# One layer norm in place of two, and block roundings moved between the first projections

## The chip, the cores and the metric

The kernel runs on one core of a Trainium2 chip. The core has five engines that run side by side and meet only at semaphores: PE (TensorE, matrix products and transposes), DVE (VectorE), ACT (ScalarE), POOL (GpSimd) and SP (SyncE, which here only issues transfers). The metric is the device time of one execution in microseconds (us).

## The reference, cut to what matters

One decoder block: a gated cross-attention, then a gated mixture of experts. Only the way into the attention matters here.

```python
def _ln(x, w, b):
    mu = jnp.mean(x, axis=-1, keepdims=True)
    var = jnp.mean(jnp.square(x - mu), axis=-1, keepdims=True)
    return (x - mu) * jax.lax.rsqrt(var + EPS) * w + b          # EPS = 1e-5

def _div_clamp_fp8(x, scale):
    y = jnp.clip(x / scale, -448, 448).astype(bfloat16).astype(float32)
    return y.astype(float8_e4m3fn).astype(float32)

x = x + tanh(g_xattn[0]) * xattn(layernorm(x), ctx_2048, ...)   # layernorm: no w, b
x = x + tanh(g_ffn[0]) * ffn(layernorm(x), ...)

def xattn(hidden, cond, ...):
    ln_out = _ln(hidden, ln_w, ln_b)            # a second normalisation of a normalised row
    q  = _ln(fp8_linear(ln_out, wq,  q_in_scale))       # qx, k, v alike
    ...
```

x is 4 blocks of 256 rows of 256 columns. Every linear input is divided by a scale of its own (q, k, v, qx), rounded to bf16 and then to fp8.

## The kernel before, in words

The program is written by hand: each engine has its own instruction list, in order, and waits on semaphores. After a start, a loop of 34 steps (`for i in range(NSUB + MAXLAG)`) runs the attention, software-pipelined: step i projects the queries of sub-step i (`project_q`), scores and exponentials of i - 1, products of i - 2. Then come the router and the experts. The change touches only the start, the loop's step 0 and one place of step 2; the loop itself and what follows stay.

The start, for each of the four blocks b of x (two tiles of 128 rows):

- SP loads x (L390), fifteen vectors into rows of one tile (L401), the context (L432), the weights of the first group (L404) and eight scalars, each spread over 128 partitions (L437). All leave in this order on one queue.
- `ln_step` on DVE, for two normalisations: statistics (`bn_stats`, `bn_aggr`, L963 to L969), POOL raises the variance to -0.5 (`ln_rstd`, L506), DVE scales (L954). The order over blocks and normalisations is written out in `LN_STEPS`.
- PE turns the vectors to columns (L1412; `vectors()` on DVE takes them over, L974) and transposes the normalised block (`transpose_h`, L1370). ACT multiplies by weight and bias (`ln_out`, L661) and divides by the four scales into bf16 (`quant_y`, L671).
- `quant` on DVE rounds to fp8 with a magic number: clamp (L992), exponent bits (L993), magic (L994), add (L995). `quant_sub` on POOL subtracts the magic again, into `xq` in 32 bits (L512). Two buffers serve the four blocks (`q_y[b % 2]`), so block b waits for the subtraction of block b - 2.
- PE transposes the first weights (`fill_kv`, L1388/L1390; two banks, so the third fill waits for the first to be emptied); ACT and DVE split them into a high and a low part (`kv_hi` L684, `kv_lo` L1016; `wq_hi` L698, `wq_lo` L1030); the context likewise (`ctx_hi` L652, `ctx_lo` L1001).
- `project_kv(0, 0)` (L1441, L1450) and `project_kv(0, 1)` follow for the keys and values of block 0, `project_q(0)` (L1465) for its queries. Each is normalised by the same round: squares on ACT (L733 for keys, L740 for queries), sums on DVE (`sums`, L1068), power on POOL (`rstd_kv`, `rstd_q`, L525/L529), scaling on DVE (`scaled_kv` L1077, `scaled_q` L1088). PE transposes the result (`fill_Tq` L1479, `fill_Tk` L1491), and DVE writes the low parts of queries and keys (`qk_lo`, L1098).

Where the roundings stand in DVE's list before:

```python
sums(0, 4)
quant(1)
scaled_kv(0, 0)
wq_lo(0, 0); wq_lo(1, 0)
# step 0:  sums(key 1), quant(2), wq_lo(0, 1), scaled_kv(0, 1), wq_lo(1, 1),
#          sums(query 0), quant(3), scaled_q(0), qk_lo(keys), qk_lo(queries) ...
```

and the order in which ACT starts: `ln_out(0)`, `quant_y(0)`, `ctx_hi(0)`, `ctx_hi(1)`, four `kv_hi`, `ctx_hi(2)`, `ctx_hi(3)`, `ln_out(1)`, `quant_y(1)`, two Tanh of the gates (L715, L716), squares of the first keys, `wq_hi`, `evac_v`, `ln_out(2)`, `ln_out(3)`, `quant_y(2)`, and in step 0 `quant_y(3)`.

Of the kernel before, what the change touches and what calls it, by code (L numbers as in the profile page):

```python
# [5 lines left out]
def flamingo_kernel(nc: bass.Bass, t: dict, out: bass.AP):  # L6
# [4 lines left out]
    ALU = mybir.AluOpType  # L11
# [4 lines left out]
    P = 128  # L16
# [9 lines left out]
    EPS = 1e-5  # L26
# [18 lines left out]
    with ctx:  # L45
# [340 lines left out]

        @block.sync
        def _(sp):
            for b in range(NB):
# [4 lines left out]
            for name, row in (("L0_xattn_ln_w", 0), ("L0_xattn_ln_b", 2), ("L0_xattn_q_in_scale", 4),  # L394
                              ("L0_xattn_k_in_scale", 6), ("L0_xattn_v_in_scale", 8),
                              ("L0_xattn_qx_in_scale", 10), ("L0_xattn_qln_w", 12), ("L0_xattn_qln_b", 13),
                              ("L0_xattn_qxln_w", 14), ("L0_xattn_qxln_b", 15), ("L0_xattn_kln_w", 16),
                              ("L0_xattn_kln_b", 17), ("L0_xattn_kxln_w", 18), ("L0_xattn_kxln_b", 19),
                              ("L0_xattn_proj_smooth", 20)):
                n = t[name].shape[0] // P  # L400
                sp.dma_start(vec_rows[row:row + n, :], t[name].rearrange("(r p) -> r p", p=P)).then_inc(vec_loaded, 16)  # L401
# [89 lines left out]
        def _(pool):  # L491
# [9 lines left out]
            def ln_rstd(count):  # L501

                pool.wait_ge(var8_ready, count + 1)
                b = LN_STATS[count][1]
# [61 lines left out]
            for i in range(NSUB + MAXLAG):  # L566
# [7 lines left out]
                if i == 0:  # L574
                    quant_sub(2)
# [7 lines left out]
                if i == 0:  # L583
                    quant_sub(3)
# [63 lines left out]
        def _(act):  # L648
# [62 lines left out]
            ln_out(1)  # L711
            quant_y(1)

            act.wait_ge(scal_loaded, 16 * len(SCALARS))
            nc.scalar.activation(gate[:, 0:1], scal[:, 6:7], ACT.Tanh).then_inc(gate_ready, 1)  # L715
            nc.scalar.activation(gate[:, 2:3], scal[:, 7:8], ACT.Tanh).then_inc(gate_ready, 1)  # L716
# [221 lines left out]
        def _(dve):  # L938
# [8 lines left out]
            def ln_step(scale, i, b):  # L947

                src = (x_sb, h_sb)[i]
                tiles = range(TPB * b, TPB * (b + 1))  # L950
                if scale:
                    dve.wait_ge(rstd8_ready, LN_STATS.index((i, b)) + 1)
                    for n in tiles:
                        ins = nc.vector.tensor_scalar(h_sb[:, n, :], src[:, n, :], mv[:, n, 0:1], rs8[:, n:n + 1],  # L954
                                                      ALU.subtract, ALU.mult)
                    ins.then_inc(h_ready, 1)
                else:
                    if i == 0:
                        dve.wait_ge(x_loaded[b], 16)
                    else:  # L960
                        dve.wait_ge(h_ready, [st[1:] for st in LN_STEPS if st[0]].index((0, b)) + 1)
                    for n in tiles:
                        ins = nc.vector.bn_stats(stat[:, n, :], src[:, n, :])  # L963
                    link(ins)
                    for n in tiles:
                        ins = nc.vector.bn_aggr(mv[:, n, :], stat[:, n, :])
                    link(ins)
                    nt = slice(TPB * b, TPB * (b + 1))
                    nc.vector.tensor_scalar_add(mv[:, nt, 1], mv[:, nt, 1], EPS).then_inc(var8_ready, 1)  # L969
# [17 lines left out]
            def quant(b):  # L987
# [5 lines left out]
                link(nc.vector.tensor_scalar(mg.bitcast(U16), y.bitcast(U16), 0x7F80, None, ALU.bitwise_and))  # L993
# [801 lines left out]
```

## Time and profile before

| | |
|---|---|
| median of 3 runs | 809.79 us (809.17 to 809.99) |
| the profiled execution | 810.1 us, span 808.3 us |
| busy share of the span | PE 90%, DVE 75%, ACT 58%, POOL 57% |
| mean granted PE clock | 0.967 of full |

The span runs from the first to the last instruction of the profiled execution; the time of that execution also holds what lies around it. A busy share is an average over the whole run; a stage has its own.

### The profile page before, as it was taken

How to read it: one execution, taken by the hardware profiler on the slowest of the kernel's cores; microseconds unless marked ns; L12 is line 12 of the kernel's file. 1: busy time of each engine (PE TensorE's matmuls, PEld its weight loads, DVE VectorE, ACT ScalarE, POOL GpSimd, SP SyncE). 2: the span in 40 equal slices, each digit the busy share in tenths (PEclk: the TensorE clock that was granted, in tenths of full speed). 3: DMA queues.
4: the chain of work that ended last, by engine and by line, in shares of the span. 5: the costliest groups of instructions: out<-in, count | busy, mean ns of one | idle time of the engine just before them, and what ended most of it. 6: DMA issues, size and time to landing. Idle time of an engine off the chain costs nothing.

```text
span 808.3 us, 15347 instructions
## 1 busy us (share of the span) xinstructions
PE 724.2 (90%) x4857; PEld 588.7 (73%) x4857; DVE 607.9 (75%) x1312; ACT 466.1 (58%) x1178; POOL 458.4 (57%) x592
## 2 busy tenths in 40 slices
PE   3548999899999989999998999998978788999996
PEld 2547778687888878888887788887766555777775
DVE  6866888788888878889886978988887673445544
ACT  3655767667686776768676776866654222222221
POOL 3464777666777766677775667676766223222220
PEclk9778999999999999999999999999999796999999
DMA  5320000101000010000001010000001104666661
GB/s 184 96 67 1 27 28 1 40 30 38 1 27 28 1 54 27 27 2 27 28 1 53 2 34 1 27 1 2 1 13 48 64 3 119 196 194 189 196 187 53
DMA packets 44478, 42.74 MB, mean 53 GB/s; under 512 B 3717, under 2 KB 43386, under 8 KB 44410
## 3 DMA queue, kind: packets, MB, share of 16 engines
q1 hardware_dynamic: 42874, 36.62, 14.9%
q0 software_dynamic: 1536, 5.28, 2.4%
q8 instruction: 35, 0.57, 0.3%
q14 instruction: 33, 0.27, 0.1%
HBM read 39.52 MB, written 2.37 MB: 52 GB/s over the span
## 4 chain that ended last, share of the span: by engine, by line
PE 61%; DVE 20%; issue 6%; ACT 6%; POOL 4%; SPq 2%; DMA 1%; POOLq 0%; DVEq 0%; ACTq 0%
PE out_ps L1729 9%; PE proj_ps L1465 6%; PE s_ps L1509 6%; PE pT_ps L1518 5%; PE proj_ps L1450 5%; DVE q_tok L1088 5%; PE aux_ps L1479 4%; PE aux_ps L1528 4%; PE aux_ps L1542 4%; PE proj_ps L1441 4%; PE work_ps L1721 3%; POOL rstd L529 3%; DVE pT_sb L1113 3%; DVE ss L1068 2%; PE work_ps L1743 2%
## 5 line engine op out<-in xcount | busy, mean ns | idle before, releaser
L544 POOL TENSOR_SCALAR p_sb<-p_sb,psum_row 128x256 f32<-128x256 f32 x256 | 125.1, 504 | 66.9 <-DVE psum_row L1107 65.7
L798 ACT ACTIVATE p_sb<-s_ps,negmax 128x256 f32<-128x256 f32 x256 | 118.2, 472 | 64.9 <-DVE negmax L1102 63.8
L1528 PE MATMUL aux_ps<-pT_sb,v_sb 128*128 128x512 f32 x256 | 120.7, 593 | 3.7 <-DVE pT_sb L1113 3.7
L1113 DVE COPY pT_sb<-pT_ps 128x512 f32<-128x512 f32 x128 | 87.7, 686 | 44.2 <-PE pT_ps L1518 43.8
L1509 PE MATMUL s_ps<-kT,qT 128*128 128x256 f32 x768 | 112.2, 289 | 8.3 <-DVE qT L1098 6.1
L551 POOL TENSOR_TENSOR y_bf<-y_bf,mg_bf 128x512 bf16<-128x512 bf16 x64 | 85.8, 1341 | 58.8 <-DVE mg_bf L1125 58.8
L1509 PEld LDWEIGHTS s_ps<-kT,qT 128*128 128x128 f32 x768 | 97.6, 190 | 18.4 <-issue 18.4
L1102 DVE TENSOR_REDUCE negmax<-s_ps 128x2 f32<-128x512 f32 x128 | 86.5, 683 | 5.9 <-PE s_ps L1509 5.6
L529 POOL TENSOR_TENSOR rstd<-var,minus_half 128x8 f32<-128x8 f32 (+1 forms) x64 | 86.6, 1353 | 5.5 <-POOL var L525 0.4
L554 POOL TENSOR_TENSOR catq<-y_bf,mg_bf 128x512 fp32r<-128x512 bf16 x64 | 79.5, 1242 | 5.0
L1729 PE MATMUL out_ps<-eo,onehot 128*128 128x256 f32 x512 | 74.4, 298 | 0.6 <-ACT eo L908 0.6
L1542 PE MATMUL aux_ps<-wpT,catq 128*128 128x256 f32 x512 | 69.1, 288 | 5.9 <-DVE wkvT L1019 4.8
L1518 PE MATMUL pT_ps<-ident,p_sb 128*128 128x128 f32 x512 | 72.9, 276 | 0.9 <-POOL p_sb L544 0.7
L1465 PE MATMUL proj_ps<-wqT,xq 128*128 128x256 f32 x512 | 69.6, 291 | 4.5 <-DVE k_tok L1077 4.5
L1729 PEld LDWEIGHTS out_ps<-eo,onehot 128*128 128x128 f32 x512 | 66.4, 194 | 9.9 <-issue 8.6
L638 POOL DMA_INDIRECT gx<-rows_dram,idx_cur x32 | 33.0, 1031 | 69.4 <-DVE w_slot L1312 60.0
L1465 PEld LDWEIGHTS proj_ps<-wqT,xq 128*128 128x128 f32 x512 | 66.2, 198 | 4.9 <-DVE wqT L1030 4.7
L1528 PEld LDWEIGHTS aux_ps<-pT_sb,v_sb 128*128 128x128 f32 x256 | 44.0, 190 | 35.1 <-issue 35.1
L1542 PEld LDWEIGHTS aux_ps<-wpT,catq 128*128 128x128 f32 x512 | 63.2, 190 | 6.8 <-DVE wkvT L1019 5.5
L1068 DVE TENSOR_REDUCE ss<-sq 128x8 f32<-128x1024 f32 (+1 forms) x64 | 60.5, 945 | 7.7 <-ACT sq L733 3.9
L1518 PEld LDWEIGHTS pT_ps<-ident,p_sb 128*128 128x128 f32 x512 | 60.5, 142 | 6.6 <-POOL p_sb L544 2.5
L908 ACT ACTIVATE eo<-work_ps,w_slot 128x256 fp32r<-128x256 f32 x32 | 15.1, 473 | 82.9 <-PE work_ps L1743 82.9
(180 smaller groups left out, 1406.8 us busy)
## 6 DMA issues: line engine op xcount, KB each, us to landing
w_up_a<-in_L_ffn_gate_up_proj SPq DMA_DIRECT2D x16, 384.0 KB, 3.6
w_up_b<-in_L_ffn_gate_up_proj SPq DMA_DIRECT2D x16, 384.0 KB, 3.5
wp_raw<-in_L_xattn_wproj SPq DMA_DIRECT2D x16, 256.0 KB, 2.9
w_down_a<-in_L_ffn_down_proj SPq DMA_DIRECT2D x16, 192.0 KB, 3.6
w_down_b<-in_L_ffn_down_proj SPq DMA_DIRECT2D x16, 192.0 KB, 3.6
w_raw<-in_L_xattn_w_kv_x SPq DMA_DIRECT2D x8, 256.0 KB, 4.1
w_raw<-in_L_xattn_wq SPq DMA_DIRECT2D x7, 256.0 KB, 2.7
w_raw<-in_L_xattn_wqx SPq DMA_DIRECT2D x7, 256.0 KB, 3.0
```

The lines of the kernel that those rows point to most:

```text
L529: nc.gpsimd.tensor_tensor(rstd[:, at], var8[:, at], minus_half[:, 0:w], ALU.pow).then_inc(rstd_ready, 1)
L544: ins = nc.gpsimd.tensor_scalar(p_sb[:, r, st, :], p_sb[:, r, st, :], rsum[:, r, st:st + 1], 1.0, ALU.mult, ALU.mult)
L551: nc.gpsimd.tensor_tensor(yc_bf[:, ty, :], yc_bf[:, ty, :], mg_bf[:, ty, :], ALU.add).then_inc(catq_ready, 1)
L798: ins = nc.scalar.activation(p_sb[:, r, st, :], s_ps[:, r % 2, st, :], ACT.Exp, bias=negmax[:, r, st:st + 1], accum_out=psum_row[:, r, st: ...
L1102: nc.vector.tensor_reduce(negmax[:, r, :], s_ps[:, r % 2, :, :], AX.X, ALU.max, negate=True).then_inc(max_ready, 1)
L1113: nc.vector.tensor_copy(pT_sb[:, r // 2, r % 2, :, :], pT_ps[:, r % 2, :, :]).then_inc(pT_ready, 1)
L1465: ins = nc.tensor.matmul(proj_ps[:, t, x * 256:(x + 1) * 256], xq[:, s.b, 3 * x, c, t * P:(t + 1) * P], wqT[:, s.gi, part, c, x * 256:(x + ...
L1509: ins = nc.tensor.matmul(s_ps[:, k % 2, st, :], qT[:, a, ty, h, st * P:(st + 1) * P], kT[:, b, ty, s.gi, :], start=(i == 0), stop=(i == 2))
L1518: ins = nc.tensor.transpose(pT_ps[:, r % 2, tt, st * P:(st + 1) * P], p_sb[:, r, st, tt * P:(tt + 1) * P], ident[:, :])
L1528: ins = nc.tensor.matmul(aux_ps[:, f.bank, :], v_sb[:, (2 * s.n + tt) % VRING, ty, s.gi, :], pT_sb[:, ty, :, tt, :], start=(tt == 0), stop ...
L1542: ins = nc.tensor.matmul(aux_ps[:, f.bank, tt * H:(tt + 1) * H], catq[:, s.gi, blk, tt * P:(tt + 1) * P], wpT[:, s.gi, part, blk, :], star ...
L1729: ins = nc.tensor.matmul(out_ps[:, n, :], onehot[:, u % 2, n * P:(n + 1) * P], eo[:, part, :], start=False, stop=False, skip_group_check=True)
```

## The change

- One normalisation in place of two. With v the variance of x, the second normalisation of a normalised row is the first with (v + EPS)^-0.5 replaced by (v (1 + EPS) + EPS^2)^-0.5, so statistics, power and scaling are done once per block.
- SP sends two blocks of x, seven vectors, the other two blocks, the keys' and values' weights, then the context. ACT's own queue sends the other eight vectors and the eight scalars, before ACT's first work. A one-column activation with no use of its own follows them.
- ACT does `ln_out` and `quant_y` of blocks 0 and 1 at the start, of block 2 after the context, and `ln_out(3)` ahead of the loop; the two Tanh move into step 2. `evac_v(0, 0)` goes ahead of `wq_hi`. PE transposes blocks 2 and 3 earlier.
- `quant` is cut into `quant_exponents` and `quant_round`, which stand in other places of DVE's list; those of block 3 now stand ahead of the query sums. The magic of blocks 2 and 3 is subtracted on DVE (`quant_less`) in place of POOL.

```diff
+        VECTORS = [... ln_w, ln_b, four in_scales, proj_smooth, then eight query and key vectors]
+        def load_vectors(eng, vectors):
+            for name, row in vectors:
+                n = t[name].shape[0] // P
+                eng.dma_start(vec_rows[row:row + n, :], t[name].rearrange("(r p) -> r p", p=P)).then_inc(vec_loaded, 16)
...
+            load_x(0)
+            load_x(1)
             sp.wait_ge(rows_clear, 1)
-            for name, row in ((fifteen vectors)):
-                ...
+            load_vectors(sp, VECTORS[:7])
+            load_x(2)
+            load_x(3)
...
+            load_kv(0, 0)
             sp.dma_start(ctx_raw, ...)
-            load_kv(0, 0)
             load_kv(0, 1)
             load_wq(0, wq0_raw, wq0_loaded)
-            for i, name in enumerate(SCALARS):
-                sp.dma_start(scal[:, i:i + 1], t[name].partition_broadcast(P)).then_inc(scal_loaded, 16)
... POOL
-            for count in range(7):
-                ln_rstd(count)
+            for b in range(NB):
+                ln_rstd(b)
             quant_sub(0)
-            ln_rstd(7)
...
-                if i == 0:
-                    quant_sub(2)
...
-                if i == 0:
-                    quant_sub(3)
... ACT
+            act.wait_ge(rows_clear, 1)
+            load_vectors(act, VECTORS[7:])
+            for i, name in enumerate(SCALARS):
+                act.dma_start(scal[:, i:i + 1], t[name].partition_broadcast(P)).then_inc(scal_loaded, 16)
+            act.wait_ge(memset_done, 3)
+            nc.scalar.activation(gate[:, 3:4], minus_half[:, 0:1], ACT.Identity)
             ln_out(0)
             quant_y(0)
+            ln_out(1)
+            quant_y(1)
             ctx_hi(0)
             ctx_hi(1)
...
             ctx_hi(3)
-            ln_out(1)
-            quant_y(1)
-            act.wait_ge(scal_loaded, 16 * len(SCALARS))
-            (two Tanh)
+            ln_out(2)
+            quant_y(2)
...
             squares_kv(0, 0)
+            evac_v(0, 0)
             wq_hi(0, 0)
             wq_hi(1, 0)
-            evac_v(0, 0)
-            ln_out(2)
             ln_out(3)
-            quant_y(2)
...
+                if i == 2:
+                    act.wait_ge(scal_loaded, 16 * len(SCALARS))
+                    (two Tanh)
... DVE
+            def ln_stats(b):
+                ... (bn_stats, bn_aggr of x_sb)
+                nc.vector.tensor_scalar(mv[:, nt, 1], mv[:, nt, 1], 1.0 + EPS, EPS * EPS, ALU.mult, ALU.add
+                                        ).then_inc(var8_ready, 1)
+            def ln_norm(b):
+                dve.wait_ge(rstd8_ready, b + 1)
+                ... (tensor_scalar of x_sb into h_sb, two tiles)
...
+            def quant_less(b):
+                dve.wait_ge(z_ready, b + 1)
+                dve.wait_ge(xq_ready, b)
+                nc.vector.tensor_tensor(xq[:, b, :, :, :].rearrange("p a c k -> p (a c) k"), q_y[b % 2], q_mg[b % 2],
+                                        ALU.subtract).then_inc(xq_ready, 1)
...
-            for step in LN_STEPS[:7]:
-                ln_step(*step)
+            ln_stats(0)
+            ln_stats(1)
+            ln_norm(0)
             vectors()
-            for step in LN_STEPS[7:12]:
-                ln_step(*step)
+            ln_norm(1)
+            ln_stats(2)
+            ln_stats(3)
+            ln_norm(2)
+            ln_norm(3)
             weight_scales()
-            quant(0)
+            quant_exponents(0)
+            quant_round(0)
             ctx_lo(0)
...
-            for step in LN_STEPS[12:]:
-                ln_step(*step)
...
+            quant_exponents(1)
+            quant_round(1)
             sums(0, 4)
-            quant(1)
+            quant_exponents(2)
             scaled_kv(0, 0)
             wq_lo(0, 0)
             wq_lo(1, 0)
+            quant_round(2)
             for i in range(NSUB + MAXLAG):
...
                 if i == 0:
-                    quant(2)
+                    quant_less(2)
...
+                if i == 0:
+                    quant_exponents(3)
+                    quant_round(3)
+                    quant_less(3)
                 if s0:
                     sums(q_seq(s0.a), 8)
-                if i == 0:
-                    quant(3)
... PE
             for i in range(2):
                 transpose_ctx(i)
+            transpose_h(2)
             for c, x in KV_ORDER:
                 fill_kv(c, x, 0)
             for i in range(2, 4):
                 transpose_ctx(i)
+            transpose_h(3)
...
             project_kv(0, 0)
-            transpose_h(2)
-            transpose_h(3)
```

## Rows read from the trace of the kernel before

**Rows 1.** Busy time by stage: us, then PE, PEld, DVE, ACT, POOL, clock, DMA.
```profile
0.00:68.80 68.80, 34.60 (x182) 30.74 (x182) 50.28 (x114) 37.49 (x84) 31.93 (x32) 0.85 0.33 102
```

**Rows 2.** The chain of waits in order of time: start, us, what.
```profile
15.25 3.46 DMA scal<-in_g_ffn
```

**Rows 3.** Timeline of SP's queue at the start: start, us, transfer issued.
```profile
3.19 0.25 SPq L401 DMA_DIRECT2D sq<-in_L_xattn_ln_b  x1
...
7.02 0.32 SPq L401 DMA_DIRECT2D sq<-in_L_xattn_proj_smooth  x1
...
11.76 0.60 SPq L437 DMA_DIRECT2D scal<-in_L_xattn_wq_scale  x1
```

**Rows 4.** Timeline of ACT, start to 50 us; brackets: idle before, releaser.
```profile
11.56 1.28 ACT L661 ACT_TABLE_LOAD   x1 [11.56 <-PE s_ps L1370]
12.86 1.02 ACT L661 ACTIVATE acc<-s_ps,vec 128x256 f32<-128x256 f32 x2
...
17.12 1.05 ACT L652 ACTIVATE ctxT<-pT_ps 128x512 fp32r<-128x512 f32 x2
...
33.47 0.19 ACT L715 ACTIVATE gate<-scal 128x1 f32<-128x1 f32 x1
...
33.66 0.57 ACT L733 ACTIVATE sq<-proj_ps 128x512 f32<-128x512 f32 x1
...
48.27 0.47 ACT L698 ACTIVATE wqT<-aux_ps,wscale 128x256 fp32r<-128x256 f32 x1
```

**Rows 5.** Timeline of DVE, start to 64 us.
```profile
5.75 0.73 DVE L954 TENSOR_SCALAR pT_sb<-x_sb,q_tok 128x256 f32<-128x256 f32 x2
...
19.27 0.68 DVE L992 TENSOR_SCALAR wp_raw<-wp_raw 128x2048 bf16<-128x2048 bf16 x1
...
21.44 1.22 DVE L995 TENSOR_TENSOR wp_raw<-wp_raw,qk_f 128x2048 bf16<-128x2048 bf16 x1
...
23.18 1.65 DVE L1016 SCALAR_TENSOR_TENSOR wkvT<-aux_ps,wscale,wkvT 128x256 fp32r<-128x256 f32 x4
...
28.62 1.43 DVE L1001 TENSOR_TENSOR ctxT<-pT_ps,ctxT 128x512 fp32r<-128x512 f32 x2 [0.16 <-ACT ctxT L652]
...
38.18 0.68 DVE L1077 TENSOR_TENSOR k_tok<-proj_ps,rstd 128x512 f32<-128x512 f32 x1
...
53.86 1.22 DVE L1068 TENSOR_REDUCE ss<-sq 128x8 f32<-128x1024 f32 x1 [3.85 <-ACT sq L740]
...
58.31 1.22 DVE L1088 TENSOR_TENSOR q_tok<-proj_ps,rstd 128x1024 f32<-128x1024 f32 x1
59.44 3.65 DVE L1098 TENSOR_TENSOR kT<-qk_f,kT 128x512 fp32r<-128x512 f32 x1
```

**Rows 6.** Timeline of PE, start to 60 us.
```profile
8.76 0.45 PE L1412 MATMUL proj_ps<-ident,sq 128*128 128x128 f32 x1 [8.76 <-DMA sq<-in_L_xattn_proj_smooth]
...
24.20 1.19 PE L1388 MATMUL aux_ps<-center,w_raw 128*128 128x128 f32 x4 [5.95 <-DVE wkvT L1016]
...
38.97 2.04 PE L1441 MATMUL proj_ps<-wkvT,xq 128*128 128x256 f32 x8 [2.87 <-DVE k_tok L1077]
...
59.58 1.11 PE L1479 MATMUL aux_ps<-ident,q_tok 128*128 128x128 f32 x4 [6.38 <-DVE q_tok L1088]
```

**Rows 7.** Timeline of POOL, start to 77 us.
```profile
0.75 0.20 POOL L492 MEMSET sq<- 128x128 f32 x1 [0.29 <-POOLq L1783]
...
35.69 1.46 POOL L529 TENSOR_TENSOR rstd<-var,minus_half 128x4 f32<-128x4 f32 x1
...
38.34 4.08 POOL L512 TENSOR_TENSOR xq<-v_sb,y_bf 128x2048 fp32r<-128x2048 bf16 x1 [1.19 <-DVE v_sb L995]
...
75.23 1.65 POOL L529 TENSOR_TENSOR rstd<-var,minus_half 128x8 f32<-128x8 f32 x1
```

**Rows 8.** The page's costliest groups: count, busy us, mean ns, idle before.
```profile
L638 POOL DMA_INDIRECT gx<-rows_dram,idx_cur x32 | 33.0, 1031 | 69.4 <-DVE w_slot L1312 60.0
```

**Rows 9.** Busy time by stretches of 4 us, columns as in rows 1.
```profile
56.00:60.00 4.00, 0.42 (x2) 0.42 (x3) 3.93 (x5) 0.00 (x0) 3.43 (x2) 0.50 0.17 58
```

More of the change, by code:

```diff
@@ L385, in qk_parts, with load_x @@
             return qk_f[:, 0, :], [qT[:, part, int(x == "TX"), :, :].rearrange("p a b -> p (a b)") for part in range(2)]
+        VECTORS = [("L0_xattn_ln_w", 0), ("L0_xattn_ln_b", 2), ("L0_xattn_q_in_scale", 4), ("L0_xattn_k_in_scale", 6),
+                   ("L0_xattn_v_in_scale", 8), ("L0_xattn_qx_in_scale", 10), ("L0_xattn_proj_smooth", 20),
+                   ("L0_xattn_qln_w", 12), ("L0_xattn_qln_b", 13), ("L0_xattn_qxln_w", 14), ("L0_xattn_qxln_b", 15),
+                   ("L0_xattn_kln_w", 16), ("L0_xattn_kln_b", 17), ("L0_xattn_kxln_w", 18), ("L0_xattn_kxln_b", 19)]
+        def load_vectors(eng, vectors):
+            for name, row in vectors:
+                n = t[name].shape[0] // P
+                eng.dma_start(vec_rows[row:row + n, :], t[name].rearrange("(r p) -> r p", p=P)).then_inc(vec_loaded, 16)
         @block.sync
         def _(sp):
-            for b in range(NB):
+            def load_x(b):
                 sp.dma_start(x_sb[:, TPB * b:TPB * (b + 1), :], t["x"][b, :, :].rearrange("(n p) h -> p n h", p=P)
                              ).then_inc(x_loaded[b], 16)
+            load_x(0)
+            load_x(1)
             sp.wait_ge(rows_clear, 1)
[L394 to L401, printed above, removed]
+            load_vectors(sp, VECTORS[:7])
+            load_x(2)
+            load_x(3)
             def load_rows(dst, name, row, n, done):
@@ L499, in _, with ln_rstd @@
                                         base=0, pattern=[[-1, P]], channel_multiplier=1).then_inc(const_ready, 1)
-            def ln_rstd(count):
-                pool.wait_ge(var8_ready, count + 1)
-                b = LN_STATS[count][1]
+            def ln_rstd(b):
+                pool.wait_ge(var8_ready, b + 1)
                 nt = slice(TPB * b, TPB * (b + 1))
@@ L710, in _ @@
             ctx_hi(3)
-            ln_out(1)
-            quant_y(1)
-            act.wait_ge(scal_loaded, 16 * len(SCALARS))
-            nc.scalar.activation(gate[:, 0:1], scal[:, 6:7], ACT.Tanh).then_inc(gate_ready, 1)
-            nc.scalar.activation(gate[:, 2:3], scal[:, 7:8], ACT.Tanh).then_inc(gate_ready, 1)
+            ln_out(2)
+            quant_y(2)
             def wp_hi(ty, g):
@@ L853, in _ @@
                     quant_y(3)
+                if i == 2:
+                    act.wait_ge(scal_loaded, 16 * len(SCALARS))
+                    nc.scalar.activation(gate[:, 0:1], scal[:, 6:7], ACT.Tanh).then_inc(gate_ready, 1)
+                    nc.scalar.activation(gate[:, 2:3], scal[:, 7:8], ACT.Tanh).then_inc(gate_ready, 1)
                 if s1:
@@ L945, in link @@
                 dve.wait_ge(dve_chain, chain[0])
-            def ln_step(scale, i, b):
-                src = (x_sb, h_sb)[i]
+            def ln_stats(b):
                 tiles = range(TPB * b, TPB * (b + 1))
[L951 to L957, printed above, removed]
-                    if i == 0:
[L959 to L969, printed above, removed]
+                dve.wait_ge(x_loaded[b], 16)
+                for n in tiles:
+                    ins = nc.vector.bn_stats(stat[:, n, :], x_sb[:, n, :])
+                link(ins)
+                for n in tiles:
+                    ins = nc.vector.bn_aggr(mv[:, n, :], stat[:, n, :])
+                link(ins)
+                nt = slice(TPB * b, TPB * (b + 1))
+                nc.vector.tensor_scalar(mv[:, nt, 1], mv[:, nt, 1], 1.0 + EPS, EPS * EPS, ALU.mult, ALU.add
+                                        ).then_inc(var8_ready, 1)
+            def ln_norm(b):
+                dve.wait_ge(rstd8_ready, b + 1)
+                for n in range(TPB * b, TPB * (b + 1)):
+                    ins = nc.vector.tensor_scalar(h_sb[:, n, :], x_sb[:, n, :], mv[:, n, 0:1], rs8[:, n:n + 1],
+                                                  ALU.subtract, ALU.mult)
+                ins.then_inc(h_ready, 1)
             def vectors():
@@ L985, in weight_scales, with quant_exponents @@
                 ins.then_inc(wscale_ready, 1)
-            def quant(b):
+            def quant_exponents(b):
                 y, mg = q_y[b % 2], q_mg[b % 2]
@@ L1364, in transpose_h @@
             def transpose_h(b):
-                pe.wait_ge(h_ready, [st[1:] for st in LN_STEPS if st[0]].index((1, b)) + 1)
+                pe.wait_ge(h_ready, b + 1)
                 wait(pe, yT_ready, b - 1)
```

6 lines of the change are left out of this document (2 added, 4 removed).

## The prediction, made before the changed kernel was run

> **What bounds the kernel now.** I read the stages first: up to 68.80 us PE, which elsewhere bounds this kernel, works only 34.60 us [rows 1]. So the start is a chain of hand-overs, and only the start is edited. Then the chain of waits: it goes through SP's queue, which issues one transfer after another until the last scalar leaves at 15.25, and the scalar's landing ends the wait of DVE [rows 2]. SP's own timeline shows why: 13 issues of vectors take from 3.19 to 7.02, 0.295 us each, and the scalars begin only at 11.76, 0.50 us each to 15.25 [rows 2, 3]. Last, the four engines: ACT's first work, a table load, starts at 11.56, its first `ln_out` at 12.86 and the next job at 17.12 [rows 4]; DVE rounds block 0 from 19.27 to 22.66 and only then gives PE's second half of the weights its bank, at 24.20 [rows 5, 6]; the sums of squares of the first queries start at 53.86, and their transposes at 59.58 [rows 5, 6]. The reader is to see that each start hangs on the end of another engine's work: what the change is worth is how much earlier PE starts at 59.58.
>
> **The change, step by step.** The sum is a timetable of the new order, from durations of before.
>
> *ACT free.* ACT now issues 8 vectors and 8 scalars itself, after POOL's clearing memset (0.75 + 0.20, so 1.0 [rows 7]). No row shows an issue on ACT. The nearest are SP's: 8 x 0.295 + 8 x 0.50 = 6.36, mean 0.40. The far bounds are the vectors' 0.295 for all (1.6 us less) and POOL's indirect transfers, 1.03 each [rows 8]. I take SP's, which are the same transfers. Then the table load 1.28 and a one-column activation, 0.19 like the Tanh [rows 4]: ACT is free at 1.0 + 6.36 + 1.47 = 8.8.
>
> *Does its input wait?* `ln_norm(0)` needs what it needed: 5.75 + 0.73 = 6.48 [rows 5]. The second statistics, powers and scalings, which stood between this and the transposes, are gone. PE's transpose of the vectors (0.45, at 8.76 before, 1.7 us after proj_smooth's issue at 7.02 [rows 3, 6]) now needs an issue at about 3.7, so it can run at 5.5. The four transposes of block 0 (1.11, as for four at 59.58 [rows 6]) end at 7.7. ACT's 8.8 is later and sets the start. x's third and fourth blocks, now behind seven vectors, and the context behind wk and wv are needed later still; DVE's normalisations of all four blocks end by about 12 and are covered by ACT.
>
> *First weights.* ACT runs `ln_out` and `quant_y` of two blocks: 17.12 - 12.86 = 4.26 each [rows 4], to 17.3. Two context copies, 17.12 to 18.17 before, take it to 18.4. Then `kv_hi` at once, as the scalars landed 3.5 us after their last issue at 7.3 (before: from 15.25 to 18.7 [rows 2]). The halves of a block are 0.42 each like `kv_lo`'s 1.65 for four [rows 5], so `kv_hi(0,0)` ends at 19.2, `kv_lo(0,0)` at 20.1, and PE starts at 20.25 in place of 24.20 [rows 6]: -3.95. DVE no longer rounds block 0 just before this; that sits at 13.1 to 16.5, in ACT's shadow.
>
> *First squares.* From PE's 24.20 to ACT's squares at 33.66 the same work follows: fills, copies, one `ln_out`, one `quant_y`. The two Tanhs before the squares (33.47 to 33.66 [rows 4]) are gone: -4.15, squares at 29.5. `quant_exponents(1)` and `quant_round(1)`, now ahead of the sums, start when the context subtractions end (28.62 + 1.43 - 3.95 = 26.1 [rows 5]), take 3.4 (four steps, 19.27 to 22.66 [rows 5]), end at 29.5, and are done as the squares end at 30.1. Without that cover the sums move by the difference.
>
> *First keys.* The power ended at 35.69 + 1.46 = 37.15 [rows 7], but DVE, busy with the rest of quant(1), scaled only at 38.18 [rows 5]. Now it is ready: 37.15 - 4.15 = 33.0, -5.1 for `scaled_kv(0,0)` and PE's 38.97 [rows 6], now 33.85.
>
> *Rounding block 2.* POOL's `quant_sub(1)` (4.08 [rows 7]) runs from 33.1 to 37.2. DVE's copy of the keys with both inputs in SBUF took 3.65 us beside POOL's last such subtraction, 59.44 to 63.09, where a normal one is 0.68 [rows 5]: I let `quant_round(2)` wait until 37.2 and end at 39.1. `sums` follow to 39.8. Then `quant_less(2)`, new on DVE. Its wait for `quant_sub(1)` is over by then; behind it in the queue are `wq_lo(0,1)`, `scaled_kv(0,1)` and so `project_q(0)`. Its price is in no row. Below it is the addition of the same size in bf16, 1.22; above it POOL's 4.08. It writes 32 bits, so I take the 32-bit rate: 0.68 for 512 and 1.22 for 1024 elements [rows 5], 0.54 per 512, so 2.3 for 2048. It ends at 42.1. POOL's small power waits behind it (1.3 more), `scaled_kv(0,1)` ends at 44.1.
> The Trainium skill ("VectorE: DVE Perf Modes", What auto-detection actually checks) lets a two-input operation go at double rate only if every tensor is 16 bits wide, and so sides with 2.3; at 1.22 the sum would be 1.2 us better.
>
> *Rounding block 3.* ACT's second half of the query weights starts at 48.27 [rows 4], 5.1 earlier at 43.2, done at 44.0: about level with DVE. DVE's `wq_lo(1,1)` ends at 45.0, the roundings of block 3 at 48.4, `quant_less(3)` at 50.7, and all of this is now ahead of the query sums. They start at 50.7 in place of 53.86: the gain falls from 5.1 to 3.2. But nothing stands behind them: the sums end at 51.9, the power takes 2.15 with its preparation (1.65 undisturbed [rows 7]), `scaled_q(0)` starts at 54.05 in place of 58.31 [rows 5]. So -4.3, and PE's 59.58 becomes 55.3. From there the same loop follows. The 3.65 us of the keys disappears, but PE projected in those microseconds, so I count nothing for it.
>
> *Tanh in the loop.* The two Tanhs return in step 2, ahead of the query's first half, on ACT's way: +0.2.
>
> Sum: -4.1. Against the profiled execution (810.1; span 808.3 and 1.8 around it) 806.0; the median shown is 0.3 lower, so **805.7**. A measurement here can tell about 0.2%, 1.6 us, from no change.
>
> **Rivals.**
> 1. *ACT's issues are dear (the other side).* ACT's start sets the chain, so each extra microsecond counts fully. It matches before at 0.40 + 4.1/16 = 0.65 us per issue and is slower by 0.2% from 0.75 on. At POOL's 1.03 [rows 8] it is 16 x 0.63 = 10.1 worse: 815.8. [...] Against: the same descriptors from SP at 0.295 to 0.50. At a middling 0.6 it ends at 808.9, no change.
> 2. *Transfers, not issues, set the start.* If the vectors still land for a transpose at 8.76, ACT starts after 8.76 + 0.45 + 1.11 = 10.3, 1.5 later: 807.2. Against: SP's issues follow back to back, and the landing is 1.7 us after the last one. The Trainium skill ("DMA: Bandwidth & Descriptors", Issuing engines are not separate DMA queues) speaks for it: two issuing engines share the same transfer engines and save only issue time, usually small; here the rows show issue time of 12 us on SP, so I give it little.
> 3. *DVE's subtraction costs what POOL's did.* 4.08 in place of 2.3, twice on the way: +3.6, 809.3, no change. At 1.22 it is 1.1 to 1.2 better: 804.5.
> 4. *The clock.* PE's granted clock is 0.50 from 56 to 60 [rows 9], half of full, that is 1.2 in place of 2.4 GHz, after an idle stretch of 6 us before 59.58. I keep that: PE's wait before 55.3 is as long. If the tighter start kept it at 2.4 GHz, the two groups of transposes and the first projection would halve, about 1.5: 804.2. A loss of the same size would come from a projection that falls to the lower clock: 807.2.
>
> **How the numbers follow.** As summed, with the small clock shifts, 0.60; rival 2 0.10; a cheaper subtraction or a kept clock 0.15; rival 1 0.12, of which 0.08 to 0.6 or 0.7 us per issue, no change or near it, and 0.04 slower; rival 3's dear end 0.03. Faster takes the first three and 0.02 of the dear issues' lower part: 0.87; same 0.09; slower 0.04. The range leaves out the dear ends (0.11 above) and some of a double gain below (0.05): from 803.4, where the cheap subtraction and a kept clock come nearly together, to 808.4, where an issue costs 0.57 us.
>
> **What would show it.** In the changed profile: ACT's table load ends by 8.7 and `quant_y(0)` begins by 10; PE's second half of the weights near 20.3, the squares near 29.5, DVE's two subtractions near 2.3 us each, query sums near 50.7 and PE's first query transposes near 55.3; everything after by the same offset. The prediction is wrong if ACT's `ln_out(0)` comes after 12.9, if DVE's subtractions exceed 4 us, or if the offset at PE's query transposes isn't that of the end.

## The result and the profile after

The changed kernel took **802.85 us** (median of 4 runs, 801.96 to 804.23) against 809.88 for the kernel before on the same chip (4 runs): ratio 0.9923, 95% interval 0.9912 to 0.9935. It is faster by 7.0 us, where 4.1 were forecast. The profiled execution took 801.96 us, span 800.1, mean granted clock of PE 0.977 of full speed (before 0.967).

The stage in which the change lies, and another stretch further on, of the changed kernel (the row of 68.80 us answers to [rows 1], the next to [rows 9]; columns as there):

```profile
0.00:68.80 68.80, 36.66 (x211) 32.53 (x212) 49.87 (x93) 39.11 (x88) 22.66 (x30) 0.90 0.32 102
...
52.00:56.00 4.00, 1.51 (x7) 1.51 (x8) 1.82 (x2) 0.29 (x1) 1.18 (x1) 0.50 0.00 0
...
554.00:556.00 2.00, 2.00 (x19) 2.00 (x18) 1.38 (x4) 0.52 (x2) 1.44 (x4) 1.00 0.00 0
```

In the same 68.80 us PE does 211 products in place of 182. At its query transposes (52 to 56) it still has half the clock, 1.2 in place of 2.4 GHz.

The chain of waits of the changed kernel, in order of time, answers to [rows 2]; the scalars have left it, and the context's transfer stands in it:

```profile
6.11 8.63 DMA p_sb<-in_ctx
...
47.64 2.29 DVE xq L1005
```

SP's queue, then ACT's queue and ACT itself (answer to [rows 3] and [rows 4]):

```profile
3.73 0.32 SPq L391 DMA_DIRECT2D sq<-in_L_xattn_proj_smooth  x1
6.11 0.53 SPq L436 DMA_DIRECT2D p_sb<-in_ctx  x1
```

```profile
0.98 0.52 ACTq L391 DMA_DIRECT2D sq<-in_L_xattn_qln_w  x1
...
7.22 0.58 ACTq L700 DMA_DIRECT2D scal<-in_g_ffn  x1
7.83 1.28 ACT L702 ACT_TABLE_LOAD   x1 [7.83 <-issue]
...
9.23 1.00 ACT L656 ACTIVATE acc<-s_ps,vec 128x256 f32<-128x256 f32 x2
...
17.71 1.05 ACT L647 ACTIVATE ctxT<-pT_ps 128x512 fp32r<-128x512 f32 x2
...
28.74 0.58 ACT L732 ACTIVATE sq<-proj_ps 128x512 f32<-128x512 f32 x1
```

Sixteen issues on ACT take from 0.98 to 7.83, 0.43 each (forecast 0.40); `ln_out(0)` starts at 9.23 in place of 12.86. DVE (answer to [rows 5]):

```profile
34.50 2.33 DVE L998 TENSOR_SCALAR qk_f<-qk_f 128x2048 bf16<-128x2048 bf16 x1
38.60 2.28 DVE L1005 TENSOR_TENSOR xq<-wp_raw,qk_f 128x2048 fp32r<-128x2048 bf16 x1
...
47.64 2.29 DVE L1005 TENSOR_TENSOR xq<-v_sb,y_bf 128x2048 fp32r<-128x2048 bf16 x1
49.85 1.21 DVE L1082 TENSOR_REDUCE ss<-sq 128x8 f32<-128x1024 f32 x1
53.21 1.23 DVE L1102 TENSOR_TENSOR q_tok<-proj_ps,rstd 128x1024 f32<-128x1024 f32 x1 [2.15 <-POOL rstd L528]
54.35 0.68 DVE L1112 TENSOR_TENSOR kT<-qk_f,kT 128x512 fp32r<-128x512 f32 x1
57.18 0.69 DVE L1112 TENSOR_TENSOR qT<-qk_f,qT 128x512 fp32r<-128x512 f32 x1 [2.15 <-ACT qT L782]
```

PE (answer to [rows 6]; the last row belongs to step 29 of the loop) and POOL ([rows 7]):

```profile
6.75 0.45 PE L1431 MATMUL proj_ps<-ident,sq 128*128 128x128 f32 x1 [6.75 <-DMA sq<-in_L_xattn_proj_smooth]
...
14.79 1.97 PE L1398 MATMUL pT_ps<-ident,p_sb 128*128 128x128 f32 x8 [4.95 <-DMA p_sb<-in_ctx]
20.88 0.68 PE L1407 MATMUL aux_ps<-center,w_raw 128*128 128x128 f32 x4 [0.73 <-DVE wkvT L1027]
...
33.12 1.61 PE L1462 MATMUL proj_ps<-wkvT,xq 128*128 128x256 f32 x8 [4.08 <-DVE k_tok L1091]
...
54.49 1.12 PE L1500 MATMUL aux_ps<-ident,q_tok 128*128 128x128 f32 x4 [7.58 <-DVE q_tok L1102]
56.11 1.83 PE L1462 MATMUL proj_ps<-wkvT,xq 128*128 128x256 f32 x8
57.78 1.55 PE L1471 MATMUL proj_ps<-wkvT,ctxT 128*128 128x512 f32 x6
...
553.91 2.05 PE L1486 MATMUL proj_ps<-wqT,xq 128*128 128x256 f32 x16
```

```profile
32.21 4.07 POOL L512 TENSOR_TENSOR xq<-v_sb,y_bf 128x2048 fp32r<-128x2048 bf16 x1
38.89 2.06 POOL L524 TENSOR_SCALAR var<-ss 128x4 f32<-128x4 f32 x1 [2.61 <-DVE ss L1082]
```

POOL's indirect transfers, [rows 8], are the same (mean 1031 ns). To see where the time comes from, lay one event of every step of the loop beside its twin: the start of DVE's scaling of the queries, `scaled_q`. Before, it starts at 58.31 in step 0, 76.92 in step 1, 547.94 in step 28 and 602.62 in step 31. The changed kernel is 5.10 earlier in step 0, 6.67 in step 1, 6.39 in step 28, 7.84 in step 29 and 7.89 in step 31. So there are three portions: 5.1 us up to the first queries, 1.6 in step 1, and 1.45 in step 29, 500 us from anything edited. The base of these differences is one execution of the kernel before, of 810.1 us; its executions in the batches below go from 807.75 to 811.11, so a number in them can be a microsecond away from a difference of medians. The last portion shows in the kernel before as this projection (the same 16 products that take 2.05 above), and the stretch around it:

```profile
560.30 3.12 PE L1465 MATMUL proj_ps<-wqT,xq 128*128 128x256 f32 x16
```

```profile
560.00:562.00 2.00, 2.00 (x15) 2.00 (x15) 1.26 (x6) 0.91 (x4) 1.58 (x4) 0.73 0.00 0
562.00:564.00 2.00, 2.00 (x11) 2.00 (x11) 0.65 (x2) 0.55 (x1) 1.78 (x2) 0.50 0.00 0
```

Same order, same work, but clock 0.73 and 0.50 where the changed kernel had 1.00.

### The profile page after: what moved, and what is told of

It reads as the page before. It is cut to its first block, busy times and chain, and to the rows that moved or that the text cites. A ratio compares the mean times of both kernels' runs of the same rounds, so it can differ in the third digit from the quotient of the medians.

```text
span 800.1 us, 15318 instructions
## 1 busy us (share of the span) xinstructions
PE 718.0 (90%) x4857; PEld 582.8 (73%) x4857; DVE 604.1 (76%) x1286; ACT 466.1 (58%) x1179; POOL 447.4 (56%) x586
## 4 chain that ended last, share of the span: by engine, by line
PE 63%; DVE 18%; ACT 6%; issue 6%; POOL 4%; DMA 1%; SPq 1%; POOLq 0%; DVEq 0%; ACTq 0%
PE out_ps L1748 9%; PE s_ps L1530 6%; PE proj_ps L1486 6%; PE proj_ps L1471 6%; PE pT_ps L1539 5%; DVE q_tok L1102 5%; PE aux_ps L1549 4%; PE aux_ps L1500 4%; PE aux_ps L1563 4%; PE proj_ps L1462 4%; PE work_ps L1740 3%; POOL rstd L528 3%; DVE pT_sb L1127 3%; DVE ss L1082 3%; PE work_ps L1762 2%
## 5 line engine op out<-in xcount | busy, mean ns | idle before, releaser
L633 POOL DMA_INDIRECT gx<-rows_dram,idx_cur x32 | 33.0, 1031 | 69.0 <-DVE w_slot L1331 59.8
L1486 PE MATMUL proj_ps<-wqT,xq 128*128 128x256 f32 x512 | 67.0, 284 | 4.0 <-DVE k_tok L1091 4.0
L1486 PEld LDWEIGHTS proj_ps<-wqT,xq 128*128 128x128 f32 x512 | 63.6, 191 | 4.3 <-issue 4.3
L760 ACT ACTIVATE qk_f<-aux_ps,vec 128x512 f32<-128x512 f32 x64 | 49.8, 778 | 23.6 <-PE aux_ps L1500 21.0
```

The source lines that it names most:

```text
L1486: ins = nc.tensor.matmul(proj_ps[:, t, x * 256:(x + 1) * 256], xq[:, s.b, 3 * x, c, t * P:(t + 1) * P], wqT[:, s.gi, part, c, x * 256:(x + ...
```

## The experiments

The first theory: the new issue order (scalars off the end of SP's list) gives nearly all of the first portion, the second normalisation and the roundings' places nothing, and the other portions are TensorE's clock. In the table "earlier by" is the start of `scaled_q` in the kernel before minus that of the run, in us, from each run's profile; the medians of before stand in brackets.

| run | median, us | ratio, 95% | earlier by: step 0 | step 1 | step 28 | step 31 |
|---|---|---|---|---|---|---|
| changed kernel | 802.85 (809.88) | 0.9923, 0.9912 to 0.9935 | 5.10 | 6.67 | 6.39 | 7.89 |
| e1 | 809.16 (809.01) | 1.0, 0.9991 to 1.001 | 0.04 | 0.01 | 0.00 | 0.00 |
| e2 | 805.22 (809.01) | 0.9956, 0.994 to 0.9971 | 4.96 | 5.49 | 5.46 | 5.42 |
| e3 | 805.25 (809.01) | 0.9958, 0.9942 to 0.9974 | 5.11 | 5.75 | 5.50 | 5.44 |
| e4 | 802.12 (809.01) | 0.9911, 0.9896 to 0.9926 | 6.91 | 7.74 | 7.45 | 7.42 |
| e5 | 804.47 (809.26) | 0.9932, 0.9919 to 0.9944 | 4.95 | 5.17 | 4.97 | 4.96 |
| e6 | 802.97 (809.26) | 0.9926, 0.9913 to 0.994 | 4.49 | 6.14 | 5.93 | 7.44 |
| e7 | 806.35 (809.26) | 0.9968, 0.9955 to 0.998 | 2.56 | 4.26 | 3.98 | 5.45 |
| e8 | 803.18 (809.26) | 0.9923, 0.9911 to 0.9935 | 6.92 | 7.33 | 7.06 | 7.04 |
| e9 | 801.54 (809.11) | 0.9901, 0.9887 to 0.9914 | 7.09 | 8.17 | 7.92 | 7.92 |
| e10 | 799.38 (809.11) | 0.9882, 0.9867 to 0.9898 | 7.01 | 9.98 | 9.76 | 11.25 |
| e11 | 804.63 (809.11) | 0.9939, 0.992 to 0.9957 | 3.01 | 4.39 | 4.06 | 5.54 |

**e1: one normalisation alone**, in the order of before.

```diff
-        LN_STEPS = [(0, 0, 0), (0, 0, 1), (1, 0, 0), (0, 1, 0), (1, 0, 1), (0, 1, 1), ...]
+        LN_STEPS = [(0, 0, 0), (0, 0, 1), (1, 0, 0), (1, 0, 1), (0, 0, 2), (0, 0, 3), (1, 0, 2), (1, 0, 3)]
...
-                    nc.vector.tensor_scalar_add(mv[:, nt, 1], mv[:, nt, 1], EPS)
+                    nc.vector.tensor_scalar(mv[:, nt, 1], mv[:, nt, 1], 1.0 + EPS, EPS * EPS, ALU.mult, ALU.add)
...
```

> The kernel before with only its two normalisations made one; transfers, orders and roundings stay. Theory (the issue order holds the start): ACT could begin about 1 us sooner, but DVE's weight scales still wait for the last scalar, landing at 18.7, and the rounding of block 0 and the first weights stand behind them. PE's second half of the weights stays at 24.2 (within 0.3) and the time at 809.9, no change. Rival (the dropped normalisation is the gain): PE's 24.2 comes 2 us or more earlier and the time is 807.9 or less.

809.16 against 809.01: nothing. DVE only waits longer for the last scalar (4.13 us in place of 2.86), and the weight scales come at 18.70 (18.74 before). So the work that gave the change its name was covered.

**e2: the issue order alone.** The kernel before with SP's new order, and vectors and scalars issued by ACT ahead of its work; all else as before.

```diff
...
+            load_vectors(act, VECTORS[7:])
+            for i, name in enumerate(SCALARS):
+                act.dma_start(scal[:, i:i + 1], t[name].partition_broadcast(P)).then_inc(scal_loaded, 16)
...
```

> The kernel before with only the new issue order: SP's list, ACT's sixteen issues, the early one-column activation; both normalisations and the old places of the roundings stay. Theory: the scalars land by 13.4, but the second normalisation of block 0 still ends at 10.3, so ACT starts at 11.5; rounding of block 0 runs from 15.9 to 19.3, PE's second half of the weights starts at 21.0 in place of 24.2, and the rest follows by 3.2: 806.7. Rival (transfers, not issues, set the start): within 0.5 of 809.9. Rival (the normalisation is the gain): the same.

4.96 at step 0, as much as the first portion of the changed kernel, and 3.8 us in the median; 3.2 were expected. The second half of the weights came about where it was expected (21.24); 1.8 more came between it and the squares, which start 7.64 behind it, at 28.88, in place of 9.46. PE's second half of the weights, at 24.20 before [rows 6]:

```profile
21.24 0.68 PE L1399 MATMUL aux_ps<-center,w_raw 128*128 128x128 f32 x4 [1.66 <-DVE wkvT L1027]
```

**e3: the roundings in their old places**, the rest of the change in.

```diff
                 if s0:
                     sums(q_seq(s0.a), 8)
+                if i == 0:
+                    quant_exponents(3)
+                    quant_round(3)
...
+                if i == 0:
+                    quant_sub(2)   # and (3), on POOL as before
```

> The changed kernel with the roundings of blocks 1 to 3 back in their old places on DVE and the subtractions of blocks 2 and 3 back on POOL. Theory (the gain is made by 28.7, where the first squares start 4.9 earlier than before, and the new places of the roundings bring about nothing, since the two subtractions on DVE stand ahead of the query sums): PE's first query transposes at 54.5 to 55.0 against 54.49, the time within 1 us of the changed kernel's 802.9, the clock permitting. Rival (the roundings in the gaps bring a good part): 2 to 3 us slower, 805 to 806.

Query transposes at 54.48, as in the changed kernel at 54.49. DVE in this run:

```profile
48.75 1.22 DVE L1086 TENSOR_REDUCE ss<-sq 128x8 f32<-128x1024 f32 x1 [2.86 <-ACT sq L743]
...
54.34 3.65 DVE L1116 TENSOR_TENSOR kT<-qk_f,kT 128x512 fp32r<-128x512 f32 x1
```

The sums come 1.1 us earlier than in the changed kernel (49.85), then the rounding of block 3 stands between them and the scaling. Up to the transposes, moving it ahead of the sums only moved the delay. At step 31, too, this profile (5.44) lies between the two of the changed kernel (7.89, and 4.96 in e5). But the times don't bear out that the places bring nothing: 805.25 lies where the rival had it, and the ratio's interval lies apart from the changed kernel's first and barely touches that of e5. The profile is that of the fastest of the six executions (804.36) and doesn't show where 2 us or more could go, so this stays open.

**e4: the subtraction of block 3 on POOL**, behind `rstd_q(0)`, in place of DVE.

```diff
                     quant_round(3)
-                    quant_less(3)
...
                 if s0:
                     rstd_q(s0)
+                if i == 0:
+                    quant_sub(3)
```

> The changed kernel with the subtraction of block 3 alone back on POOL, behind the power of the first queries. Theory (this subtraction is on the way to the query sums): sums at 47.6 in place of 49.85, PE's first query transposes near 52.2 in place of 54.49, and the time 2.2 less, 800.6. DVE's low part of the keys is then held until POOL's subtraction ends near 55, as before; PE is projecting meanwhile, so it costs nothing. Rival (the held DVE gives it back): the scores wait, and the time stays within 0.5 of 802.9.

```profile
52.68 1.12 PE L1501 MATMUL aux_ps<-ident,q_tok 128*128 128x128 f32 x4 [5.17 <-DVE q_tok L1104]
```

Transposes at 52.68, 1.81 earlier. So the 2.3 us of DVE ahead of the sums stand on the chain, as the forecast had them. The time gained less than expected: 802.12, against 802.85 and 804.47 (e5) of the changed kernel.

**e5: the changed kernel again.**

> The changed kernel itself, run beside the others of this call, as their measure and as a second profile. Its steps up to PE's first query transposes hang on hand-overs alone and should come within 0.1 us of the first profile (54.49). The theory that the 8.2 us between the two profiles' spans are 5.1 of hand-overs and the rest clock expects another profile to differ, if at all, only in stretches where the granted clock differs, by up to 1.5 us each; the median stays within 1 us of 802.9.

The same program, with nothing edited, keeps the first portion (4.95) and loses nearly all of the other two. The key projection, 1.83 and 1.55 above, and the projection of step 29, 2.05 above:

```profile
58.12 2.71 PE L1471 MATMUL proj_ps<-wkvT,ctxT 128*128 128x512 f32 x6
```

```profile
555.33 3.40 PE L1486 MATMUL proj_ps<-wqT,xq 128*128 128x256 f32 x16
```

So 2.9 us of the first profile's 7.9 are not in the program's order: they come and go between executions.

**e6: products to keep PE busy.** Four products of no use (`x_sb` by the identity, into a bank that is free; nothing reads the result) ahead of the query transposes of step 0.

```diff
+                if i == 0:
+                    for k in range(4):
+                        nc.tensor.matmul(pT_ps[:, k % 2, :, :]..., ident[:, :],
+                                         x_sb[:, 0:2, :]..., start=True, stop=True)
                 if s0:
                     fill_Tq(s0, 0)
```

> The changed kernel with four products of no use on PE while it waits for the first queries (47 to 54.5), into a PSUM tile that is free then. Theory (the lower clock after that wait costs the chain): PE's first transposes still start at 54.5, but run at the higher clock, 0.6 each in place of 1.1, the second key projection 2.7 in place of 3.4, and the second scaled queries come 1.2 to 1.7 earlier: about 801.5. Rival (the transposes and the projection are covered by ACT and DVE): no change, 802.9 within 0.4.

```profile
47.51 3.68 PE L1654 MATMUL pT_ps<-x_sb,ident 128*128 128x512 f32 x8
...
55.10 1.11 PE L1500 MATMUL aux_ps<-ident,q_tok 128*128 128x128 f32 x4 [3.91 <-DVE q_tok L1102]
```

The expectation failed: PE is idle another 3.91 us behind them, and the transposes take 1.11, as without them.

**e7: scalars last on SP again**, the rest of the change in.

```diff
+            for i, name in enumerate(SCALARS):
+                sp.dma_start(scal[:, i:i + 1], t[name].partition_broadcast(P)).then_inc(scal_loaded, 16)
             sp.wait_ge(aux_filled, Fill("KV", 1, 1, 0).filled)
... (and the same loop taken from ACT)
```

> The changed kernel with the eight scalars alone issued last on SP again, as before. Theory (the place of the scalars in the issue order holds the start): ACT starts about 1 us sooner, but the weight scales come at 19.3, the rounding of block 0 and the first weights behind them; PE's second half of the weights at 24.2 in place of 20.9, its first query transposes 3.3 later, near 57.8: 806.2, all but the last part of the gain lost. Rival (sooner vectors, the single normalisation and the new places of the roundings make the gain): less than 1 us lost.

The scales and PE's second half:

```profile
17.00 0.62 DVE L983 TENSOR_SCALAR wscale<-vec,scal 128x2 f32<-128x2 f32 x4 [4.59 <-DMA scal<-in_g_ffn]
```

```profile
22.46 1.19 PE L1407 MATMUL aux_ps<-center,w_raw 128*128 128x128 f32 x4 [5.62 <-DVE wkvT L1027]
```

Half of the first portion goes (2.56 left of 5.10), less than expected, as the scalars landed for 17.00 and not for 19.3. Part of what is left is the same cause: with eight vectors gone from SP's queue, the scales come 1.74 sooner than before (18.74), and so does PE's second half (24.20 to 22.46). The ratio's interval lies apart from the changed kernel's.

**e8: e4 with products of no use**, three ahead of the query transposes and five of half the size in step 29 (nothing reads the results).

```diff
+                if i == NSUB - 3:
+                    pe.wait_ge(pT_ready, s1.m - 1)
+                    for k in range(5):
+                        nc.tensor.matmul(pT_ps[:, 0, 0, :], ident[:, :], x_sb[:, NT - 1, :], start=True, stop=True)
...
```

> The changed kernel with the subtraction of block 3 on POOL (1.8 us sooner at the first queries in the run of that edit) and products of no use in two waits of PE: three ahead of the first query transposes, five of half the size in step 29, where the granted clock fell in the profiles before and after that edit and cost 1.5 us. Theory (both are clock after a wait): the second scaled queries 8.5 to 9.5 earlier than in the kernel before, the same or 1.5 more at the end, 800 or less. Rival (the clock's fall there is not set by this wait): step 29 loses 1.5 us again, 801.5.

```profile
52.54 3.43 DVE L1114 TENSOR_TENSOR kT<-qk_f,kT 128x512 fp32r<-128x512 f32 x1
```

```profile
52.67 0.66 PE L1501 MATMUL aux_ps<-ident,q_tok 128*128 128x128 f32 x4 [2.45 <-DVE q_tok L1104]
...
60.72 1.24 PE L1531 MATMUL s_ps<-kT,qT 128*128 128x256 f32 x6 [2.38 <-DVE qT L1114]
61.76 3.35 PE L1487 MATMUL proj_ps<-wqT,xq 128*128 128x256 f32 x16
```

Now the transposes are at the higher clock, 0.66. But the gain is given back: PE waits 2.38 us for DVE, whose low part of the keys runs beside POOL's subtraction (3.43 us, 0.68 in the changed kernel), and behind that wait it projects at the lower clock, 3.35. Step 1 is no better than e4's. In step 29 the run gains 1.46 (from 7.06 to 8.52) and is back at 7.04 by step 31: there the same projection takes 3.04, where it takes 2.06 in e7 behind the same wait of 2.15. With 803.18, where 800 or less was expected, the theory failed on the time.

**e9: the subtraction of block 3 later on DVE**, in the 2.15 us in which DVE waits for ACT (last DVE row of the changed kernel above).

```diff
                     quant_round(3)
-                    quant_less(3)
...
                     qk_lo(s0.n, "TKs")
+                if i == 0:
+                    quant_less(3)
```

> The changed kernel with DVE's subtraction of block 3 moved from ahead of the query sums to behind the low part of the first keys, into a gap of 2.15 us that DVE has there. Theory (the subtraction ahead of the sums is a term of 2.3 us on the chain, and it needs nobody's place): query sums at 47.6 and PE's query transposes at 52.2 in place of 54.5, and no engine's work beside DVE's low part of the keys, which stays at 0.68; about 2 us better than the changed kernel of the same clock, 800.5 to 802.5. Rival (the 2.3 us only move behind the transposes, where the low part of the queries then waits): PE's first scores no earlier than in the changed kernel, and nothing gained. Rival of the clock: gain at the transposes, part of it lost again in the key projection, 0.7 as with the subtraction on POOL.

```profile
47.85 1.22 DVE L1082 TENSOR_REDUCE ss<-sq 128x8 f32<-128x1024 f32 x1 [0.32 <-ACT sq L739]
...
52.36 0.68 DVE L1112 TENSOR_TENSOR kT<-qk_f,kT 128x512 fp32r<-128x512 f32 x1
52.96 2.28 DVE L1005 TENSOR_TENSOR xq<-v_sb,y_bf 128x2048 fp32r<-128x2048 bf16 x1
55.19 0.69 DVE L1112 TENSOR_TENSOR qT<-qk_f,qT 128x512 fp32r<-128x512 f32 x1
```

The theory held: the 2.28 fill the gap, the low part of the queries follows at 55.19 with no wait, and step 0 is 2.0 to 2.1 earlier than in the two profiles of the changed kernel.

**e10: e9 with three products of no use** ahead of the query transposes (nothing reads the results).

> The kernel with the later subtraction of block 3, and three matrix products of no use on PE ahead of the query transposes, in the stretch in which PE waits. Theory (what the transposes and the key projection run at is the granted clock, and it falls in PE's idle stretch): transposes at 52.2 at the higher clock, about 0.66 for four, key projection near 1.1 and 1.6, and, since no subtraction on POOL now holds DVE's low part of the keys, PE's first scores without the wait of 2.4 us that the busy variant with POOL's subtraction had; projection of the next queries near 2.1; another 1 to 1.5 us better at step 1 than the later subtraction alone. Rival: PE waits for the low part of the queries instead, and the clock's gain is given back as before.

PE of e10, then the same rows of e9:

```profile
52.58 0.66 PE L1501 MATMUL aux_ps<-ident,q_tok 128*128 128x128 f32 x4 [2.44 <-DVE q_tok L1102]
...
53.43 1.19 PE L1463 MATMUL proj_ps<-wkvT,xq 128*128 128x256 f32 x8
54.46 1.57 PE L1472 MATMUL proj_ps<-wkvT,ctxT 128*128 128x512 f32 x6
```

```profile
52.50 1.12 PE L1501 MATMUL aux_ps<-ident,q_tok 128*128 128x128 f32 x4 [5.31 <-DVE q_tok L1102]
...
54.12 2.06 PE L1463 MATMUL proj_ps<-wkvT,xq 128*128 128x256 f32 x8
55.97 1.85 PE L1472 MATMUL proj_ps<-wkvT,ctxT 128*128 128x512 f32 x6
```

Same start, but 1.8 us less to the end of the key projection, and the same 1.8 between the two runs at step 1 (9.98 and 8.17). Nothing gives it back here. At 799.38 this is the fastest of all; its interval lies below those of both comparisons of the changed kernel. Of its 11.25 at step 31, 1.45 belong to step 29, where this profile happened to have the higher clock. Its four executions fall in two pairs, as that would give: 798.62 and 798.68 with a mean granted clock of 0.982, 800.09 and 800.66 with 0.975.

**e11: transposes of block 2 ahead of the context's**, since PE waits for the context.

```diff
+            transpose_h(2)
             for i in range(2):
                 transpose_ctx(i)
-            transpose_h(2)
```

> The changed kernel with PE's transposes of block 2 ahead of those of the context's first half, for whose landing PE waits to 14.79. Theory (the transfer of the context, issued at 6.11 and used at 14.79, is on the chain, and 1.1 us of PE's work that stands behind it could be done before): PE's second half of the weights up to 1 us earlier than 20.88, if ACT's copies of the context are not what sets it; 0.3 to 0.8 us better at the query transposes. Rival (ACT, which ends its work on block 1 at about 17.7, sets the weights, not the context): second half at 20.8 to 20.9 and nothing gained.

The rival held. The context landed at 15.44 here and the second half came at 21.39, 5.95 later; in the changed kernel 6.09 later (14.79, 20.88). ACT's copy of the context starts as ACT ends its work on block 1, and `kv_hi` follows without a pause:

```profile
15.36 3.31 ACT L666 ACTIVATE v_sb<-acc,rvec 128x256 bf16<-128x256 f32 x8
18.57 1.05 ACT L647 ACTIVATE ctxT<-pT_ps 128x512 fp32r<-128x512 f32 x2
19.52 0.46 ACT L679 ACTIVATE wkvT<-aux_ps,wscale 128x256 fp32r<-128x256 f32 x1
```

PE's next work then ran longer (the eight transposes of the context's second half 1.92, in e9 1.04), and step 0 lost 2.1 against the changed kernel. Whether the order or the execution did that is open. The time, 804.63, is close to the 804.47 of e5.

## Why the prediction was right, and where its size was off

**Direction and mechanism: right in the main.** That the order of issues held the start, e2 shows: that edit alone gives 4.96 of 5.10 at step 0. e7 takes the scalars back and loses half. That ACT's start sets the chain, as "ACT free" and rival 1 had it, is not shown: in e2 ACT's first `ln_out` comes at 11.60, 2.4 later than in the changed kernel, and PE's second half of the weights only 0.36 later. The size was off: 802.85 lies 0.55 below the range that was given (803.4 to 808.4), the 804.47 of e5 inside it. And the last sign of being wrong came true in the first profile: the offset at PE's query transposes, 5.1, isn't that of the end, 7.9. In e5 the two agree (4.9 and 5.0).

**Step by step.** ACT's start was forecast at 8.8 and came at 9.23 (0.43 per issue, and the vectors' and scalars' issues begin at 0.98). PE's second half: 20.25, came at 20.88. I had put the context "needed later still"; it landed at 14.79, so ACT waited twice on PE for the first halves, 0.6 together, and up to here the chain runs over that transfer and PE, not over ACT as the sum had it. Squares: 29.5, came at 28.74. Here I let "the same work" follow as before, 9.46 less the Tanhs' 0.19; it took 7.86, 1.4 less, and PE's first fill took 0.68 in place of 1.19, behind a wait of 0.73 in place of 5.95. That two errors, 0.6 late and 1.4 early, partly cancel is luck. First keys 33.85, came at 33.12. The hold of `quant_round(2)` by POOL to about 37 came (2.33 in place of 0.69), the subtractions took 2.28 and 2.29 (forecast 2.3), POOL's small operation was held (2.06). The Trainium skill ("VectorE: DVE Perf Modes", What auto-detection actually checks) sided with 2.3 and the trace agrees. Query sums 50.7, came at 49.85; transposes 55.3, came at 54.49, so -5.1 in place of -4.3, 54.64 in e5. The Tanh's +0.2: the gain falls by 0.28 from step 1 to step 28 in the first profile, 0.20 in e5, and by 0.03 in e2, where the Tanhs stand in their old place.

**The term that failed: the clock, counted at nothing.** "As summed, with the small clock shifts" had no term for it, and rival 4 put a kept clock at 1.5 us, in step 0 only. Measured were the start's fills and what hangs on them (the 1.4 above, within the first portion), step 1 (1.6 in the first profile, 0.2 in e5) and step 29 (1.45, and 0 in e5). So the changed kernel's gain is 5.0 us that belong to its order and up to 2.9 that vary from run to run; with the spread of the kernel before, this is how the medians lie 7.0 and 4.8 below before. e10 shows what the clock is worth at step 1: with PE given work until 2.44 us before the transposes, they and the key projection run at the higher clock, and step 1 comes 1.8 earlier than in e9. Why two executions of one program differ at the same place stays open, for step 1 as for step 29: PE's wait ahead was nearly the same in both profiles (7.58 and 7.37, 2.42 and 2.41).

**Rivals.** 1 (dear issues) fell with 0.43 each, 0.50 at most in the other runs (e4: sixteen in 8.00). 2 (transfers set the start) mostly fell: the vectors' transpose came at 6.75, neither the 5.5 forecast nor 8.76, and was hidden behind ACT's issues. 3 (the subtraction costs what POOL's did) fell with 2.28. The Trainium skill ("DMA: Bandwidth & Descriptors", Issuing engines are not separate DMA queues) calls the issue time that a second issuing engine saves usually small relative to the transfer itself. For one scalar the trace agrees (0.50 us of issue, 3.46 of transfer [rows 2, 3]); for a list of 34 in a row it doesn't: the issue order is worth 5 us at step 0 (e2).

**What the change left.** Its rounding of block 3 ahead of the sums brought nothing over the old place up to the query transposes (e3); whether it does in the time is open. The cost was there as forecast, 2.3 us of DVE on the chain, and e9 takes it off.

## What to carry to other kernels

Read what each queue issues before the first useful instruction: a transfer that is small and last in a list can hold the whole start, and sending it from an engine that has most of that time to spare (ACT starts at 9.23, and without the scalars, in e7, at 7.99) was worth more here than dropping half the normalisation. Moving work from behind a step to ahead of it gained nothing at the next step (e3), as both lie on the same chain; look for the gap in the same engine's timeline that is as long as the work (2.15 us for 2.28). And compare two profiles of the same program before crediting a difference of 1 or 2 us to an edit.

## What the runs showed of the hardware that was not expected

- The granted clock differs between executions of one program at the same place: 16 products of step 29 took 2.05 us in one profile of the changed kernel and 3.40 in the other. In step 0, PE had the lower clock behind an idle stretch of 7.58, 5.31 or 3.91 us, and the higher behind one of 2.44 or 2.45 with products just before it. The wait alone doesn't settle it: that of step 29 is 2.42 and 2.41 in these two profiles.
- A gain in clock can be lost to the next wait: in e8 PE came faster to a value that was not ready, waited 2.38 us, and the next 16 products took 3.35, where e10, without that wait, projected in 2.13.
- The last scalar's issue on ACT took 0.58 us in the first profile, 0.85 in e5, 1.34 in e11 and 1.55 in e4, and moved ACT's start with it (table load at 7.83, 8.20, 8.68, 8.98). In e7, with no scalars on ACT's queue, the context landed at 12.66, in place of 14.79 to 15.61 in the other runs with the new order. That the scalars' transfers slow the context's was not tried by itself.
- The engines do not meet only at semaphores, as the section on the chip has it. DVE's step of the rounding at 34.50 took 2.33 us beside POOL's subtraction (32.21 to 36.28), in place of 0.69, its low part of the keys 3.65 in place of 0.68 (e3, 54.34), and POOL's small operation at 38.89 took 2.06 beside DVE's subtraction, where the one before it, at 30.26, took 0.43.
